# Software-pipelining the layer norm and transpose loop of a transformer layer on eight cores

## The chip, the cores and the metric

The kernel runs as one program on the 8 cores of a Trainium2 chip, without communication between the cores. The metric is the device time in microseconds of the slowest core. Each core has its own engines: TensorE (PE, with weight loads shown as PEld), VectorE (DVE), ScalarE (ACT), GpSimd (POOL, which here only issues the weight DMAs) and SyncE (SP, which issues the loads of activations and constants).

## What is computed

One transformer layer: attention on a layer norm of x, then a gated feed-forward network on a layer norm of the result, each with a residual. The reference, cut to what matters here:

```python
def _layernorm(x, axis=-1, eps=1e-5):
    m = jnp.mean(x, axis=axis, keepdims=True)
    v = jnp.var(x, axis=axis, keepdims=True)
    return (x - m) / jnp.sqrt(v + eps)

    x = L0_attn_x                       # (4, 2048, 2048) f32
    x = x + _L0_attn_ref(_layernorm(x, axis=-1), Wq, Wk, Wv, Wo)   # 16 heads, 4 KV heads, rope, alibi, causal
    x = x + _L0_ffn_ref(_layernorm(x, axis=-1), ...)               # router over 64, 8 groups, silu(g) * u, down
    return x
```

Each core takes one batch element and half of its 128-row query blocks. It normalises all 2048 tokens of its batch element, since it needs K and V of all of them.

## The kernel before

The program is written as lists of instructions per engine, which a small class collects: `p.emit` and `p.inc` append an instruction to an engine's list ("te", "ve", "se", "gp", "sy"), `p.inc` also increments that engine's semaphore and returns the count reached, `p.wait` makes an engine wait for such a count, and `p.dma` issues a load (its line in the profile is always L182). Each engine works its list strictly in the order of the calls, so the order in which `build` is written is the order of every queue.

The stages are: layer norm and transposition of x into XLN (bf16, features on the partitions); the K projection with rope (L436), the V projection (L491), the Q projection (L542); attention (`build_p2`); the output projection and the second layer norm (`build_p3`, which loads half of x_perm once more and transposes it); the feed-forward network over 8 groups (`build_p4`), which ends with transposes and stores (L1299).

The change touches the first stage alone. It runs over 16 tiles `tt` of 128 tokens, each in two halves `hc` of 1024 features. There are four load buffers XL of 128 x 1024 f32, so two tiles; half hc of tile tt uses XL[(2*tt + hc) % 4]. The columns of the small statistics are kept four-fold (`par = tt % 4`). For each tile, in the order of the queues:

- SP loads both halves, once VectorE has normalised out of that buffer and ScalarE's Exp of that tile is done (`ve_xl_free`, `se_xl_free`).
- ScalarE sums each half (L338, Copy with accumulate); VectorE squares and accumulates each half (L344).
- VectorE makes mean and variance in five instructions on one column (L349, L352, L355, L358, L361).
- ScalarE makes 1/sqrt(var + eps) as Ln (L366) and Exp (L369); VectorE makes -mean times that (L372).
- For each half: VectorE normalises it into XLNORMP[par % 2] (L382), TensorE transposes it in eight blocks of 128 x 128 f32 into PS[2 + hc] (L392), and ScalarE casts the result into XLN (L401, a CAST row). XLNORMP has two buffers, but a tile uses the one picked by its parity for both of its halves, so the second half is normalised after the first half's transposes. VectorE also waits for the transposes behind each half.

The K projection needs the casts of four tiles for each of its four column blocks (`evac_done`), and its weights in WKV, which POOL loads (two of four before the first stage ends).

Of the kernel before, what the change touches and what calls it, by code (L numbers as in the profile page):

```python
# [189 lines left out]
def build(taps=(), upto=4, sub=99):  # L190
    nc = bass.Bass("TRN2", target_bir_lowering=False)
# [21 lines left out]
    out = nc.dram_tensor("out", [TOWN, D], F32, kind="ExternalOutput").ap()  # L213
# [7 lines left out]
    def f32v(off_b, n):  # L221
# [19 lines left out]
    XL   = [f32v(163840, 1024), f32v(167936, 1024),  # L241
            f32v(65536, 1024), f32v(69632, 1024)]
# [12 lines left out]
    XLNORMP = [f32v(192512, 1024), f32v(196608, 1024)]  # L255
# [9 lines left out]
    IDNF  = f32v(cst(512), 128)  # L265
# [13 lines left out]
    SCR  = f32v(cst(256), 64)  # L279
# [4 lines left out]
    p = Prog(nc)  # L284
# [17 lines left out]
    se_xl_free = [0, 0, 0, 0]  # L302
    te_norm_free = [0, 0]
    cS0, cS1, cQ0, cQ1, cSUM, cSQ, cM, cMSQ, cVAR, cR, cNMR, cTMP = range(12)
    cEPS = 62

    def scr(col):
        return SCR[:, col:col + 1]
# [9 lines left out]
    prev_nv_tok = [0, 0]  # L318
    tpose_done = []
    evac_done = []  # L320
    last_norm_te = 0
    for tt in range(16):
        par = tt % 4
        def scr(col, par=None, _S=SCR):
            return _S[:, col:col + 1]
        def scrp(col, par):
            return SCR[:, 12 * par + col:12 * par + col + 1]
        for hc in (0, 1):
            slot = (tt * 2 + hc) % 4
            p.wait("sy", "VE", ve_xl_free[slot])  # L330
            p.wait("sy", "SE", se_xl_free[slot])
            xld.append((f"LX{slot}", p.dma("sy", XL[slot], x_r[tt, hc], sem=f"LX{slot}")))
        for hc in (0, 1):
            slot = (tt * 2 + hc) % 4
            p.wait("se", *xld[tt * 2 + hc])
            p.wait("se", "VE", prev_ve_tok[par])
            p.wait("se", "SE", prev_sq_tok[par])
            rtok = p.inc("se", lambda s_, sl=slot, par=par, c=(cS0, cS1)[hc]: s_.activation(  # L338
                HJUNK, XL[sl], AF.Copy, accum_out=scrp(c, par)), "SE")
            prev_sq_tok[par] = rtok  # L340
            p.wait("ve", *xld[tt * 2 + hc])
            p.wait("ve", "VE", prev_rtok[par])
            sq_tok = p.inc("ve", lambda v, sl=slot, par=par, c=(cQ0, cQ1)[hc]:
                v.scalar_tensor_tensor(  # L344
                    out=VJUNK, in0=XL[sl], scalar=1.0, in1=XL[sl],
                    op0=ALU.mult, op1=ALU.mult, accum_out=scrp(c, par)), "VE")
            prev_rtok[par] = sq_tok
        p.wait("ve", "SE", rtok)
        t1 = p.inc("ve", lambda v, par=par: v.tensor_tensor(  # L349
            out=scrp(cSUM, par), in0=scrp(cS0, par), in1=scrp(cS1, par), op=ALU.add), "VE")  # L350
        p.wait("ve", "VE", sq_tok)
        t2 = p.inc("ve", lambda v, par=par: v.tensor_tensor(  # L352
            out=scrp(cSQ, par), in0=scrp(cQ0, par), in1=scrp(cQ1, par), op=ALU.add), "VE")
        p.wait("ve", "VE", t1)
        t3 = p.inc("ve", lambda v, par=par: v.tensor_scalar(out=scrp(cM, par), in0=scrp(cSUM, par),  # L355
                   scalar1=1.0 / D, scalar2=None, op0=ALU.mult), "VE")
        p.wait("ve", "VE", t3)
        t4 = p.inc("ve", lambda v, par=par: v.tensor_scalar(out=scrp(cMSQ, par), in0=scrp(cM, par),  # L358
                   scalar1=scrp(cM, par), scalar2=None, op0=ALU.mult), "VE")
        p.wait("ve", "VE", t4)  # L360
        ve_tok = p.inc("ve", lambda v, par=par: v.scalar_tensor_tensor(  # L361
            out=scrp(cVAR, par), in0=scrp(cSQ, par), scalar=1.0 / D, in1=scrp(cMSQ, par),
            op0=ALU.mult, op1=ALU.subtract), "VE")
        prev_ve_tok[par] = ve_tok
        p.wait("se", "VE", ve_tok)
        s1 = p.inc("se", lambda s_, par=par: s_.activation(scrp(cTMP, par), scrp(cVAR, par), AF.Ln,  # L366
                   bias=scr(cEPS)), "SE")
        p.wait("se", "SE", s1)
        se_tok = p.inc("se", lambda s_, par=par: s_.activation(scrp(cR, par), scrp(cTMP, par), AF.Exp,  # L369
                       scale=-0.5), "SE")  # L370
        p.wait("ve", "SE", se_tok)
        ve_tok = p.inc("ve", lambda v, par=par: v.tensor_scalar(  # L372
            out=scrp(cNMR, par), in0=scrp(cM, par), scalar1=scrp(cR, par), scalar2=-1.0,
            op0=ALU.mult, op1=ALU.mult), "VE")
        p.wait("ve", "VE", ve_tok)
        p.wait("se", "VE", ve_tok)
        for hc in (0, 1):
            slot = (tt * 2 + hc) % 4
            se_xl_free[slot] = se_tok
            p.wait("ve", "TE", te_norm_free[par % 2])  # L380
            p.wait("ve", "VE", prev_nv_tok[par % 2])
            nv_tok = p.inc("ve", lambda v, sl=slot, par=par: v.tensor_scalar(  # L382
                out=XLNORMP[par % 2], in0=XL[sl], scalar1=scrp(cR, par), scalar2=scrp(cNMR, par),
                op0=ALU.mult, op1=ALU.add), "VE")
            prev_nv_tok[par % 2] = nv_tok
            ve_xl_free[slot] = nv_tok
            p.wait("te", "VE", nv_tok)
            ps = PS[2 + hc]
            if len(evac_done) >= 2:
                p.wait("te", "SE", evac_done[-2])  # L390
            for j in range(8):
                fn = (lambda t_, j=j, ps=ps, par=par: nc.tensor.transpose(  # L392
                    ps[:, j * 128:(j + 1) * 128],
                    XLNORMP[par % 2][:, j * 128:(j + 1) * 128], IDNF))
                if j == 7:
                    te_norm_free[par % 2] = p.inc("te", fn, "TE")
                else:
                    p.emit("te", fn)
            p.wait("ve", "TE", te_norm_free[par % 2])
            p.wait("se", "TE", te_norm_free[par % 2])  # L400
            ev = p.inc("se", lambda s_, ps=ps, hc=hc, tt=tt: s_.copy(  # L401
                out=XLN.rearrange("p (hh q) -> p hh q", q=2048)[:, hc * 8:hc * 8 + 8,
                    tt * 128:(tt + 1) * 128],
                in_=ps.rearrange("p (a b) -> p a b", b=128)), "SE")
            evac_done.append(ev)
    p1a_te = p.cnt["TE"]; p1a_ve = p.cnt["VE"]
    taps_avail["XLN"] = (XLN, BF16, "SE", p.cnt["SE"])
    q_rope_done = kv_rope_done = 0
# [2 lines left out]
    if sub >= 1:  # L411
# [11 lines left out]
        for c in range(4):  # L423
            slot = c % 2
# [6 lines left out]
            for tc in range(4):  # L431
                if c == 0:
                    p.wait("te", "SE", evac_done[(tc * 4 + 3) * 2 + 1])
                ps = PS[tc // 2]
                for hh in range(16):
                    fn = (lambda t_, hh=hh, tc=tc, ps=ps, sl=slot: nc.tensor.matmul(  # L436
                        ps[:, (tc % 2) * 512:(tc % 2) * 512 + 512],
                        WKV[sl][:, hh * 128:(hh + 1) * 128],
                        XLN[:, hh * 2048 + tc * 512: hh * 2048 + tc * 512 + 512],
                        start=(hh == 0), stop=(hh == 15)))  # L440
# [5 lines left out]
            for ch in range(2):  # L446
                psK = PS[ch]
                psW = PS[2 + ch]
                sl = slice(ch * 1024, ch * 1024 + 1024)
# [4 lines left out]
                se_tok = p.inc("se", lambda s_, psK=psK: s_.copy(out=RAW, in_=psK[:]), "SE")  # L454
# [3 lines left out]
                for half_ in range(2):  # L458
                    fn = (lambda t_, psW=psW, half_=half_: nc.tensor.matmul(
                        psW[:, half_ * 512:half_ * 512 + 512], JROT,  # L460
                        RAW[:, half_ * 512:half_ * 512 + 512], start=True, stop=True))
# [5 lines left out]
                    out=VTTF[:, 0:1024], in0=RAW, in1=COS2K[:, sl], op=ALU.mult), "VE")  # L467
                p.wait("ve", "TE", jtok)
                sm_tok = p.inc("ve", lambda v, psW=psW, sl=sl: v.tensor_tensor(
                    out=VTTF[:, 1024:2048], in0=psW[:], in1=SIN2K[:, sl], op=ALU.mult), "VE")  # L470
                p.wait("ve", "VE", sm_tok)
                ev = p.inc("ve", lambda v, c=c, sl=sl: v.tensor_tensor(
                    out=KT[:, c * 2048 + sl.start: c * 2048 + sl.stop],
                    in0=VTTF[:, 0:1024], in1=VTTF[:, 1024:2048], op=ALU.add), "VE")
# [5 lines left out]
        for c in range(4 if sub >= 2 else 0):  # L480
            slot = c % 2
# [6 lines left out]
            for tc in range(4):  # L488
                ps = PS[tc // 2]
                for hh in range(16):  # L490
                    fn = (lambda t_, hh=hh, tc=tc, ps=ps, sl=slot: nc.tensor.matmul(  # L491
                        ps[:, (tc % 2) * 512:(tc % 2) * 512 + 512],
                        WKV[sl][:, hh * 128:(hh + 1) * 128],
                        XLN[:, hh * 2048 + tc * 512: hh * 2048 + tc * 512 + 512],
                        start=(hh == 0), stop=(hh == 15)))
# [11 lines left out]
            for grp in (0, 1):  # L507
                ps = PS[2 + grp]
                for j in range(8):
# [6 lines left out]
                    else:  # L516
# [3 lines left out]
                    out=VTOK.rearrange("p (tt f) -> p tt f", f=512)[:, grp * 8:grp * 8 + 8,  # L520
                        c * 128:(c + 1) * 128],
# [9 lines left out]
        for h in range(NH if sub >= 3 else 0):  # L531
            slot = h % 2
# [805 lines left out]
```

How the kernel before makes its waits and increments, by code:

```python
    def inc(self, eng, fn, sem, n=1):  # L165
        self.cnt[sem] += n
        h = self.sem[sem]
        self.ops[eng].append(lambda e, fn=fn, h=h, n=n: fn(e).then_inc(h, n))
        return self.cnt[sem]
# [1 line left out]
    def wait(self, eng, sem, val):  # L171
        if val <= 0:
            return
        h = self.sem[sem]
        self.ops[eng].append(lambda e, h=h, v=val: e.wait_ge(h, v))
```

## Time and profile before

| | us |
|---|---|
| median of 2 runs | 3482.24 (3478.38 to 3486.09) |
| profiled execution | 3484.57 |
| its span on the slowest core (core 2) | 3483.0 |
| spans of the other cores | 3459.6 to 3471.1 |
| TensorE, busy in the span | 2939.4 (84%) |
| VectorE | 1045.2 (30%) |
| ScalarE | 432.8 (12%) |
| GpSimd | 385.3 (11%) |

The page divides the span into 40 slices of 87 us. TensorE is busy 2, 3 and 5 tenths in the first three and mostly 7 to 9 tenths after that. In the rows, a time such as 203.37 is us from the start of the span, the number behind it is the duration, "xN" the number of instructions merged into a row, and the bracket tells how long the engine stood idle before the row and what ended the wait. L numbers are lines of the kernel before. AR is the one large SBUF tensor that all buffers are cut from, PS is PSUM. Rows are of core 2, the slowest, unless a group names another. Of the matmul records a few per cent can be missing, so a merged matmul row can have a count that is short by one or two.

### The profile page before, as it was taken

How to read it: one execution, taken by the hardware profiler on the slowest of the kernel's cores; microseconds unless marked ns; L12 is line 12 of the kernel's file. 1: busy time of each engine (PE TensorE's matmuls, PEld its weight loads, DVE VectorE, ACT ScalarE, POOL GpSimd, SP SyncE). 2: the span in 40 equal slices, each digit the busy share in tenths (PEclk: the TensorE clock that was granted, in tenths of full speed). 3: DMA queues.
4: the chain of work that ended last, by engine and by line, in shares of the span. 5: the costliest groups of instructions: out<-in, count | busy, mean ns of one | idle time of the engine just before them, and what ended most of it. 6: DMA issues, size and time to landing. Idle time of an engine off the chain costs nothing.

```text
span 3483.0 us, 33988 instructions; the slowest of 8 cores (3459.6 to 3483.0 us)
## 1 busy us (share of the span) xinstructions
PE 2939.4 (84%) x12367; PEld 1317.6 (38%) x12602; DVE 1045.2 (30%) x1358; ACT 432.8 (12%) x663; POOL 385.3 (11%) x350
## 2 busy tenths in 40 slices
PE   2356787788765997899999999999999999999986
PEld 1222332122233456343443443443443433434434
DVE  2433134433452125313214114123123123133123
ACT  2320011233453110000000000000000000000000
POOL 0000010000000100111111111111111111111110
PEclk9998897555786995899999999999999999999997
DMA  5312264000002620787676676776775876776744
GB/s 130 88 36 25 19 60 46 1 1 13 1 1 85 67 24 5 69 80 68 65 73 67 67 78 59 69 77 63 73 73 55 81 71 60 73 74 63 76 46 122
DMA packets 640647, 200.52 MB, mean 58 GB/s; under 512 B 632027, under 2 KB 632540, under 8 KB 639206
## 3 DMA queue, kind: packets, MB, share of 16 engines
q0 software_dynamic: 628208, 159.67, 47.6%
q1 hardware_dynamic: 12278, 38.67, 3.8%
q8 instruction: 105, 1.72, 0.2%
q14 instruction: 56, 0.46, 0.1%
HBM read 349.57 MB, written 8.39 MB: 103 GB/s over the span
## 4 chain that ended last, share of the span: by engine, by line
PE 73%; DMA 9%; DVE 8%; issue 5%; ACT 4%; DVEq 0%; SPq 0%; ACTq 0%; POOLq 0%
PE PS L1215 17%; PE PS L1209 17%; PE PS L1260 13%; DMA AR<-downT 6%; PE PS L542 3%; DVE AR L779 3%; PE PS L768 3%; PE PS L773 2%; PE PS L869 2%; PE PS L436 2%; PE PS L392 2%; PE PS L491 2%; PE PS L960 2%; PE PS L1169 1%; DMA AR<-x_perm 1%
## 5 line engine op out<-in xcount | busy, mean ns | idle before, releaser
L1209 PE MATMUL PS<-AR 128*128 128x512 bf16 x2759 | 826.2, 379 | 4.9 <-DVE AR L1176 1.9
L1215 PE MATMUL PS<-AR 128*128 128x512 bf16 x2760 | 826.4, 379 | 3.0
L1260 PE MATMUL PS<-AR 128*128 128x512 bf16 x2755 | 649.0, 390 | 39.6 <-DMA AR<-downT 25.5
L1260 PEld LDWEIGHTS PS<-AR 128*128 128x128 bf16 x2816 | 273.3, 100 | 416.2 <-issue 127.2
L1234 DVE TENSOR_TENSOR AR<-PS,AR 128x1024 bf16<-128x1024 f32 x88 | 107.7, 1224 | 1009.1 <-ACT AR L1229 1009.1
L1209 PEld LDWEIGHTS PS<-AR 128*128 128x128 bf16 x2816 | 275.7, 98 | 335.1 <-issue 3.5
L1215 PEld LDWEIGHTS PS<-AR 128*128 128x128 bf16 x2816 | 275.7, 98 | 333.1 <-issue 1.4
L1229 ACT ACTIVATE AR<-PS 128x1024 bf16<-128x1024 f32 x88 | 90.1, 1024 | 1811.7 <-PE PS L1215 1811.7
L1272 DVE TENSOR_TENSOR AR<-AR,PS 128x1024 f32<-128x1024 f32 x128 | 156.3, 1221 | 468.7 <-PE PS L1260 468.7
L768 PE MATMUL PS<-AR 128*128 128x512 bf16 (+3 forms) x355 | 153.2, 433 | 101.7 <-DVE AR L756 99.8
L747 ACT ACTIVATE AR<-PS,AR 128x384 bf16<-128x384 f32 (+3 forms) x365 | 198.5, 577 | 306.3 <-PE PS L717 127.5
L182 POOL DMA_DIRECT2D AR<-gateT x88 | 100.8, 1145 | 1032.9 <-PE PS L1215 1022.8
L182 POOL DMA_DIRECT2D AR<-downT x128 | 137.1, 1071 | 666.4 <-PE PS L1169 484.9
L392 PE MATMUL PS<-AR 128*128 128x128 f32 x256 | 62.1, 424 | 160.4 <-DVE AR L382 141.9
L773 PE MATMUL PS<-AR 128*128 128x512 bf16 (+3 forms) x363 | 162.1, 451 | 5.6 <-DVE PS L731 3.3
L1176 DVE TENSOR_TENSOR AR<-PS,AR 128x1024 bf16<-128x1024 f32 x128 | 154.3, 1217 | 3.5 <-PE PS L1169 3.3
L756 DVE TENSOR_TENSOR AR<-AR 128x128 bf16<-128x128 bf16 x365 | 75.7, 223 | 248.3 <-ACT AR L747 246.4
L869 PE MATMUL PS<-AR 128*128 128x512 bf16 x501 | 113.3, 383 | 5.2 <-DMA AR<-Wo 4.4
L542 PE MATMUL PS<-AR 128*128 128x512 bf16 x502 | 115.3, 386 | 2.2 <-DVE AR L519 1.7
L768 PEld LDWEIGHTS PS<-AR 128*128 128x128 bf16 x365 | 39.9, 109 | 201.9 <-issue 194.6
L779 DVE RECIPROCAL AR<-PS 128x512 f32<-128x512 f32 x32 | 107.4, 3357 | 26.8 <-PE PS L773 26.8
L392 PEld LDWEIGHTS PS<-AR 128*128 128x128 f32 x256 | 50.2, 223 | 171.9 <-issue 171.9
(124 smaller groups left out, 1848.2 us busy)
## 6 DMA issues: line engine op xcount, KB each, us to landing
AR<-gateT POOLq DMA_DIRECT2D x88, 512.0 KB, 6.3
AR<-upT POOLq DMA_DIRECT2D x88, 512.0 KB, 8.2
AR<-downT POOLq DMA_DIRECT2D x128, 352.0 KB, 5.3
AR<-x_perm SPq DMA_DIRECT2D x48, 512.0 KB, 4.5
AR<-Wq POOLq DMA_DIRECT2D x16, 512.0 KB, 8.5
AR<-Wo POOLq DMA_DIRECT2D x16, 512.0 KB, 6.5
out<-AR SPq DMA_DIRECT2D x8, 1024.0 KB, 3.9
AR<-Wk POOLq DMA_DIRECT2D x4, 512.0 KB, 9.0
```

The source lines that it names most:

```text
L182: return self.inc(q, lambda e, o=out, i=in_: e.dma_start(out=o, in_=i), sem, 16)
L392: fn = (lambda t_, j=j, ps=ps, par=par: nc.tensor.transpose(ps[:, j * 128:(j + 1) * 128], XLNORMP[par % 2][:, j * 128:(j + 1) * 128], IDNF))
L542: fn = (lambda t_, hh=hh, tc=tc, ps=ps, sl=slot: nc.tensor.matmul(ps[:, tc * 512: tc * 512 + 512], WSL[sl][:, hh * 128:(hh + 1) * 128], XL ...
L747: ncols=ncols, sl6=sl6: s_.activation(PSB[sl6][:, 0:ncols], scs[:, 0:ncols], AF.Exp, bias=ALIBIK[:, h * 16 + kp: h * 16 + kp + 1], scale=C ...
L768: ncolsj=ncolsj, first=first, last=last: nc.tensor.matmul(OS[:, 128 * sj:512], VTOK[:, (kpj * 4 + kv) * 128:(kpj * 4 + kv + 1) * 128], PSB ...
L773: ncolsj=ncolsj, first=first, last=last: nc.tensor.matmul(OS[:, 512 + 128 * sj:1024], ONESBF, PSB[sl4j][:, 0:ncolsj], start=first, stop=la ...
L779: r1 = p.inc("ve", lambda v, OS=OS: v.reciprocal(out=RECIPB, in_=OS[:, 512:1024]), "VE")
L869: fn = (lambda t_, dh=dh, tc=tc, ps=ps, sl=slot: nc.tensor.matmul(ps[:, tc * 512:tc * 512 + 512], WSL[sl][:, dh * 128:(dh + 1) * 128], OT[ ...
L1209: fn = (lambda t_, hh=hh, tc=tc, psG=psG, sl=sg: nc.tensor.matmul(psG[:, tc * 512:(tc + 1) * 512], GSL[sl][:, hh * 128:(hh + 1) * 128], XG ...
L1215: fn = (lambda t_, hh=hh, tc=tc, psU=psU, sl=su: nc.tensor.matmul(psU[:, tc * 512:(tc + 1) * 512], USL[sl][:, hh * 128:(hh + 1) * 128], XG ...
L1260: fn = (lambda t_, it=it, tc=tc, psD=psD, sl=sd: nc.tensor.matmul(psD[:, tc * 512:(tc + 1) * 512], DSL[sl][:, it * 128:(it + 1) * 128], AP ...
L1272: x2_add[hh] = p.inc("ve", lambda v, hh=hh, psD=psD: v.tensor_tensor(out=X1T[:, hh * 1024:(hh + 1) * 1024], in0=X1T[:, hh * 1024:(hh + 1) ...
```

## The change

The loop over tiles is split into four functions, and these are called in a skewed order. `emit_load` issues the loads of a tile, `emit_stats_sums` ScalarE's two sums, `emit_stats` VectorE's squares, the small statistics, Ln and Exp, and `emit_finish` the rest: -mean times rstd, the normalisation, the transposes and the casts. Step s of the new loop issues the sums of tile s, the finish of tile s-1, the loads of tile s+1, and then the statistics of tile s.

In `emit_finish` half hc is normalised into XLNORMP[hc], and both normalisations are issued before the transposes. VectorE's waits for the transposes behind each half are gone; it waits for the transposes of the tile before when it overwrites XLNORMP[hc]. TensorE waits for the cast of the tile before in the same PSUM tile (`evac_prev[hc]`), as it did. SP's wait for ScalarE before a buffer is loaded anew is now for the sum of that half and no longer for the tile's Exp; ScalarE's wait for -mean times rstd ahead of the casts is dropped.

The diff, cut to its core (the statements inside the functions that are not shown are the same):

```diff
-    for tt in range(16):
-        par = tt % 4
...
+    def emit_load(tt):
         for hc in (0, 1):
             slot = (tt * 2 + hc) % 4
             p.wait("sy", "VE", ve_xl_free[slot])
             p.wait("sy", "SE", se_xl_free[slot])
             xld.append((f"LX{slot}", p.dma("sy", XL[slot], x_r[tt, hc], sem=f"LX{slot}")))
+
+    def emit_stats_sums(tt):
+        par = tt % 4
...
+            rtok_t[tt][hc] = rtok
+            se_xl_free[slot] = rtok
+
+    def emit_stats(tt):
...
+        exp_tok[tt] = se_tok
+
+    def emit_finish(tt):
+        par = tt % 4
+        p.wait("ve", "SE", exp_tok[tt])
...
-        p.wait("ve", "VE", ve_tok)
-        p.wait("se", "VE", ve_tok)
+        p.wait("ve", "VE", nmr_tok)
         for hc in (0, 1):
             slot = (tt * 2 + hc) % 4
-            se_xl_free[slot] = se_tok
-            p.wait("ve", "TE", te_norm_free[par % 2])
-            p.wait("ve", "VE", prev_nv_tok[par % 2])
-            nv_tok = p.inc("ve", lambda v, sl=slot, par=par: v.tensor_scalar(
-                out=XLNORMP[par % 2], in0=XL[sl], scalar1=scrp(cR, par), scalar2=scrp(cNMR, par),
+            p.wait("ve", "TE", te_norm_free[hc])
+            nv_tok = p.inc("ve", lambda v, sl=slot, par=par, hc=hc: v.tensor_scalar(
+                out=XLNORMP[hc], in0=XL[sl], scalar1=scrp(cR, par), scalar2=scrp(cNMR, par),
                 op0=ALU.mult, op1=ALU.add), "VE")
-            prev_nv_tok[par % 2] = nv_tok
+            prev_nv_tok[hc] = nv_tok
             ve_xl_free[slot] = nv_tok
+        for hc in (0, 1):
+            nv_tok = prev_nv_tok[hc]
             p.wait("te", "VE", nv_tok)
             ps = PS[2 + hc]
-            if len(evac_done) >= 2:
-                p.wait("te", "SE", evac_done[-2])
+            p.wait("te", "SE", evac_prev[hc])
...
-            p.wait("ve", "TE", te_norm_free[par % 2])
-            p.wait("se", "TE", te_norm_free[par % 2])
+            p.wait("se", "TE", te_norm_free[hc])
...
+            evac_prev[hc] = ev
             evac_done.append(ev)
+
+    emit_load(0)
+    emit_load(1)
+    for step in range(17):
+        if step < 16:
+            emit_stats_sums(step)
+        if step >= 1:
+            emit_finish(step - 1)
+        if step >= 1 and step + 1 < 16:
+            emit_load(step + 1)
+        if step < 16:
+            emit_stats(step)
```

## Rows read from the trace of the kernel before

**Rows 1.** Windows view: us, busy time (instructions) of PE, PEld, DVE, ACT, POOL; clock, DMA share, GB/s.
```profile
27.67:222.70 195.03, 62.10 (x256) 50.49 (x258) 81.59 (x193) 75.99 (x129) 0.00 (x0) 1.00 0.33 84
```

**Rows 2.** Waits, 27 to 235 us: who waited for whom, us in total, times, longest.
```profile
PE PS L392 <- DVE AR L382: 141.9, 18, 36.5
ACT AR L401 <- PE PS L392: 94.6, 32, 3.8
DVE AR L382 <- PE PS L392: 39.5, 16, 2.9
DVE AR L344 <- PE PS L392: 36.3, 15, 2.5
```

**Rows 3.** Timeline, 150 to 330 us: one tile's round on core 2.
```profile
198.48 1.01 ACT L401 CAST AR<-PS 128x1024 bf16<-128x1024 f32 x1 [2.24 <-PE PS L392]
198.63 1.22 DVE L344 SCALAR_TENSOR_TENSOR AR<-AR 128x1024 f32<-128x1024 f32 x1 [2.44 <-PE PS L392]
199.39 1.06 ACT L338 ACTIVATE AR<-AR 128x1024 f32<-128x1024 f32 x1
...
199.97 1.22 DVE L344 SCALAR_TENSOR_TENSOR AR<-AR 128x1024 f32<-128x1024 f32 x1
...
200.63 1.06 ACT L338 ACTIVATE AR<-AR 128x1024 f32<-128x1024 f32 x1
201.12 0.08 DVE L344 DVE_READ_ACCUMULATOR AR<-AR 128x1 f32 x1
...
201.88 0.16 DVE L349 TENSOR_TENSOR AR<-AR 128x1 f32<-128x1 f32 x1 [0.68 <-ACT AR L338]
...
202.98 0.29 ACT L366 ACTIVATE AR<-AR 128x1 f32<-128x1 f32 x1 [1.20 <-DVE AR L361]
203.37 0.20 ACT L369 ACTIVATE AR<-AR 128x1 f32<-128x1 f32 x1
203.68 0.21 DVE L372 TENSOR_SCALAR AR<-AR 128x1 f32<-128x1 f32 x1 [0.79 <-ACT AR L369]
204.14 0.81 DVE L382 TENSOR_SCALAR AR<-AR 128x1024 f32<-128x1024 f32 x1 [0.24 <-DVE AR L372]
...
205.20 1.94 PE L392 MATMUL PS<-AR 128*128 128x128 f32 x8 [6.81 <-DVE AR L382]
207.23 1.01 ACT L401 CAST AR<-PS 128x1024 bf16<-128x1024 f32 x1 [3.66 <-PE PS L392]
...
208.45 1.94 PE L392 MATMUL PS<-AR 128*128 128x128 f32 x8 [1.31 <-ACT AR L401]
210.49 1.01 ACT L401 CAST AR<-PS 128x1024 bf16<-128x1024 f32 x1 [2.24 <-PE PS L392]
```

**Rows 4.** Timeline, core 2: the first tile's Exp and the last group of transposes.
```profile
34.95 0.20 ACT L369 ACTIVATE AR<-AR 128x1 f32<-128x1 f32 x1
...
220.54 1.94 PE L392 MATMUL PS<-AR 128*128 128x128 f32 x8 [1.39 <-ACT AR L401]
```

**Rows 5.** Timeline, core 0, 205 to 224 us: last transposes, then the K projection.
```profile
219.60 1.94 PE L392 MATMUL PS<-AR 128*128 128x128 f32 x8 [1.39 <-ACT AR L401]
...
221.34 2.84 PE L436 MATMUL PS<-AR 128*128 128x512 bf16 x7
```

**Rows 6.** Tile view of x_perm, 0 to 235 us: its 32 loads of this stage.
```profile
DMA to landing us min/median/max: 3.9/4.7/20.9
```

**Rows 7.** DMA view, 1075 to 1135 us: issues, KB each, median us to landing.
```profile
AR<-x_perm SPq DMA_DIRECT2D x14, 512.0 KB, 3.9
```

**Rows 8.** DMA view, 0 to 235 us: the K weights.
```profile
AR<-Wk POOLq DMA_DIRECT2D x2, 512.0 KB, 19.8
```

**Rows 9.** Timeline of PE: transposes in the V stage and in the output stage.
```profile
415.63 1.07 PE L511 MATMUL PS<-AR 128*128 128x128 f32 x8 [2.67 <-DVE AR L504]
...
3466.78 3.65 PE L1299 MATMUL PS<-AR 128*128 128x128 f32 x16 [2.61 <-DVE AR L1306]
```

**Rows 10.** Windows view of a part of the output stage.
```profile
3440.00:3470.00 30.00, 17.19 (x79) 15.86 (x80) 11.66 (x10) 0.00 (x0) 0.00 (x0) 0.56 0.43 179
```

More of the change, by code:

```diff
@@ L321, in build, with scr, scrp @@
     last_norm_te = 0
-    for tt in range(16):
-        par = tt % 4
[L324 to L327, printed above, removed]
+    evac_prev = [0, 0]
+    exp_tok = [0] * 16
+    rtok_t = [[0, 0] for _ in range(16)]
+    def scr(col, par=None, _S=SCR):
+        return _S[:, col:col + 1]
+    def scrp(col, par):
+        return SCR[:, 12 * par + col:12 * par + col + 1]
+    def emit_load(tt):
         for hc in (0, 1):
@@ L340, in build @@
             prev_sq_tok[par] = rtok
+            rtok_t[tt][hc] = rtok
[3 more added lines that the diff above has]
+        for hc in (0, 1):
+            slot = (tt * 2 + hc) % 4
             p.wait("ve", *xld[tt * 2 + hc])
@@ L347, in build @@
             prev_rtok[par] = sq_tok
+        rtok = rtok_t[tt][1]
         p.wait("ve", "SE", rtok)
@@ L370, in build @@
                        scale=-0.5), "SE")
-        p.wait("ve", "SE", se_tok)
-        ve_tok = p.inc("ve", lambda v, par=par: v.tensor_scalar(
+        exp_tok[tt] = se_tok
+    def emit_finish(tt):
+        par = tt % 4
+        p.wait("ve", "SE", exp_tok[tt])
+        nmr_tok = p.inc("ve", lambda v, par=par: v.tensor_scalar(
             out=scrp(cNMR, par), in0=scrp(cM, par), scalar1=scrp(cR, par), scalar2=-1.0,
             op0=ALU.mult, op1=ALU.mult), "VE")
-        p.wait("ve", "VE", ve_tok)
@@ L384, in build @@
                 op0=ALU.mult, op1=ALU.add), "VE")
-            prev_nv_tok[par % 2] = nv_tok
+            prev_nv_tok[hc] = nv_tok
             ve_xl_free[slot] = nv_tok
+        for hc in (0, 1):
+            nv_tok = prev_nv_tok[hc]
             p.wait("te", "VE", nv_tok)
             ps = PS[2 + hc]
-            if len(evac_done) >= 2:
-                p.wait("te", "SE", evac_done[-2])
+            p.wait("te", "SE", evac_prev[hc])
             for j in range(8):
-                fn = (lambda t_, j=j, ps=ps, par=par: nc.tensor.transpose(
+                fn = (lambda t_, j=j, ps=ps, hc=hc: nc.tensor.transpose(
@@ L393, in build @@
                     ps[:, j * 128:(j + 1) * 128],
-                    XLNORMP[par % 2][:, j * 128:(j + 1) * 128], IDNF))
+                    XLNORMP[hc][:, j * 128:(j + 1) * 128], IDNF))
                 if j == 7:
-                    te_norm_free[par % 2] = p.inc("te", fn, "TE")
+                    te_norm_free[hc] = p.inc("te", fn, "TE")
                 else:
                     p.emit("te", fn)
-            p.wait("ve", "TE", te_norm_free[par % 2])
-            p.wait("se", "TE", te_norm_free[par % 2])
+            p.wait("se", "TE", te_norm_free[hc])
```

## The prediction

> **What bounds the kernel now.** I read the page first: the span of 3483.0 us (3484.57 us with what lies around it) ends in matmul stages that the diff leaves alone. So I went to the stretch that the changed loop fills, from the first load's landing to the first matmul of the K projection. The row of that stretch [rows 1] is 195.03 us long, and in it TensorE is busy 62.10 us, VectorE 81.59 and ScalarE 75.99: no engine is busy for half of it, and the DMA share is 0.33. Nothing is at capacity here; the time is hand-overs. The waits of the same stretch [rows 2] say which: TensorE waits 141.9 us for the normalised halves (L382), ScalarE 94.6 us for transposes, VectorE 39.5 us for transposes before the second normalisation and 36.3 us before the next tile's squares. That is one tile at a time, going round all engines.
>
> The timeline of one tile [rows 3] shows the round. From one tile's second cast (198.48) to the next one's (210.49) is 12.01 us. In order: the sums and squares of both halves, the small statistics, Ln, Exp, -mean*rstd, normalise half 0 (204.14), transpose it (205.20), cast it (207.23), and only then the second half's transposes (208.45) and cast (210.49), because both halves share one XLNORMP buffer. The first Exp of the stage starts at 34.95 and the last group of transposes at 220.54 [rows 4]; behind that group the K projection starts without a gap, since on core 0 the next matmul starts 221.34 - 219.60 = 1.74 us after the last group did [rows 5]. So this stage's length enters the end one for one.
>
> **The change, step by step.** No arithmetic is added or dropped: the instructions are the same ones with the same shapes. What moves is (a) each half gets its own XLNORMP buffer, so both normalisations and both transpose groups follow one another; (b) ScalarE sums the next tile ahead of this tile's casts; (c) VectorE squares the next tile behind this tile's normalisations, while TensorE transposes. I place a tile's instructions from the start of the Exp of the tile before, called t = 0; every term is a start-to-start difference in [rows 3] unless another group is named.
>
> - Path through TensorE. Exp to -mean*rstd 0.31 (203.37 to 203.68); to normalise half 0: 0.46; to its transposes 1.06. So transposes of half 0 start at 1.83. The second group stands right behind it on TensorE, its input being ready: half 1 is normalised by about 0.77 + 2 x 0.81 = 2.39. A group followed by more work takes 1.74 us on core 0 [rows 5], so it starts at 3.57. Transposes to cast 2.03 (205.20 to 207.23): the second cast starts at 5.60. Cast to the next ScalarE instruction 0.91 (198.48 to 199.39): Ln at 6.51. Ln to Exp 0.39: the next Exp at 6.90.
> - Path through VectorE. The squares of the next tile start at about 2.39, the second square 1.34 later at 3.73 (198.63 to 199.97). The first of the small instructions follows the second square by 1.91 now (199.97 to 201.88), but it waits there for ScalarE's sums; the accumulator read starts 1.15 after the square (201.12) and I put the small chain at 1.25 behind the square, 4.98. Small chain to Ln 1.10 (201.88 to 202.98): 6.08. That is 0.43 before ScalarE is free, so VectorE doesn't set the period. With the whole 1.91 it would be 6.74, a period of 7.13; this is my upper bound for that step.
> - ScalarE. The two sums start at about 0.2 and 1.44 (199.39 to 200.63 is 1.24) and are read out by 2.6, before the first cast can start at 1.83 + 2.03 = 3.86. Standing ahead of the casts they cost nothing, as long as their data is there. If this cover went, each microsecond over 1.26 would hold the first cast, and over about 2 the second.
> - Loads. On SP's queue the loads of tile s+1 wait for the normalisations of tile s-1 and for its sums, as before. The first is free at about t = 1.6 and has its data after the median of 4.7 us at 6.3; it is wanted by the sum at 6.90 + 0.2 = 7.1. The second is free at 2.4, lands at 7.1 and is wanted at 8.3. The worst landing, 20.9 us, belongs to the first loads, which queue behind the constants [rows 6]. The rate asked for is 1.05 MB per 6.90 us, 152 GB/s; a later stage loads the same x_perm blocks two at a time and its 14 loads landed in 3.9 us at the median [rows 7], so I take 4.7 and not more. SP has nothing else queued in this stage.
> - POOL. It issues nothing in the stage. The K weights are now wanted some 79 us earlier, at about 144 us; their first two loads are issued ahead of the stage and took 19.8 us [rows 8]. Cost nothing.
>
> So the period falls from 12.01 to 6.90 us. Fifteen periods after 34.95 the last Exp starts at 138.45; the last group of transposes starts 3.57 later at 142.02, where it started at 220.54. The saving is 78.5 us, and since the K projection follows directly and the rest is unchanged, the profiled execution would be 3484.57 - 78.5 = 3406.1 us. The median of the runs is 2.3 us under the profiled execution, so the forecast is **3404 us**, 2.3% less.
>
> One thing could move this path: TensorE's clock. A group of eight takes 1.94 us here, 1.07 us in the V stage at 415.63 [rows 9], and the K projection's first matmuls on core 0 come about 0.43 us apart, seven in 2.84 us [rows 5], so this stage works at the lower of the two levels (1.2 GHz), though the granted clock of its stretch prints 1.00 [rows 1]. The new loop has TensorE in work some 3.66 of 6.90 us, 53%. The nearest row is the output stage: sixteen transposes in 3.65 us, 2.61 us idle, thus 58% in work, and a granted clock of 0.56, mostly the lower level [rows 9, 10]. I therefore keep the lower level. The Trainium skill ("TensorE: Matmul & The Clock Gate", Part 4: PE-mode transpose) says that transposes do not count towards the full clock as matmuls do; by that rule the sum above stands. The same page's Part 1 says that the low clock is the default and activity releases it; by that one the first rival below would hold. The output stage's row agrees more with the former.
>
> **Rivals.**
> - *The clock rises.* Both groups then take about 1.07 us, the casts are done by about 5, and VectorE's 6.08 + 0.39 = 6.47 us becomes the period. The last transposes would end near 34.95 + 15 x 6.47 + 1.83 + 2.0 = 135.8 instead of 222.5, and ten first matmuls of the K projection gain about 0.2 each: 89 us saved, 3393 us against the median. For it: the density of TensorE's work rises from a third to a half. Against it: the 0.56 at 58%.
> - *Loads become the bound.* A buffer goes free, is loaded for L, is summed (0.2 + 2.5), cast behind it (1.9), Ln and Exp (0.4 and handover), then normalised (1.6): two periods = L + 6.6. At L = 4.7 that asks only 5.7 us, and from L = 7.2 it decides. If eight cores loading at twice the density double the landing to 9.4, the period is 8.0 us, the saving 78.5 - 15 x 1.1 = 62 us, and the time 3420 us, within 2%. For it: two loads are now in flight within 0.8 us of each other. Against it: the 3.9 us in the stage with the same rate.
> - *The overlap is worth less than the starts say*, because waits on semaphores that are now spread over a shorter period take time that today hides behind others. The VectorE bound of 7.13 costs 3.5 us; a period of 7.5 costs 9 us and gives 3413 us, the border of 2%.
> - *Slower than before.* ScalarE's queue is in order, and the next tile's sums now stand ahead of this tile's casts. A late load so holds the casts, these hold PSUM and Ln, and the stage could pass 12.01 us per tile; by the same formula this needs L above 24.0 - 6.6 = 17.4 us, with 18 us it would be 12.3 us per tile and 3487 us. Only loads behind the constants took so long (20.9).
> - *The order doesn't overlap at all* would need the buffers to be shared still; the two XLNORMP halves exclude that.
>
> **How the numbers follow.** Forecast 0.72, with its own range of 3399 to 3411 (period 6.6 to 7.4). Clock rises 0.09. Loads bound or overlap worth less, past 7.4 us per tile: 0.16, most of it between 3412 and 3422. Slower 0.02, and 0.01 for anything I don't see, counted as slower. The range takes the clock's 3393 and ends at 3416. A measurement of this kernel can tell about 2% from no change, that is below 3412.6 us: faster 0.80, same 0.17, slower 0.03.
>
> **What would show it.** In the changed kernel's timeline the second casts should be 6.9 us apart; the two transpose groups of a tile touch, and the first matmul of the K projection starts near 143.8 us instead of 222. TensorE's waits for L382 should shrink from 141.9 us to about 50 and ScalarE's idle time should lie before the casts. VectorE should wait for Exp before -mean*rstd, not for TensorE. Wrong would be: ScalarE or VectorE waiting for x_perm beyond the first tile (loads), groups of eight taking 1.07 us (clock), Ln waiting for the small chain (VectorE as the bound), or later stages that differ in length.

## The result

| | before | changed |
|---|---|---|
| profiled execution | 3484.57 us | 3403.09 us |
| its span, slowest core | 3483.0 us | 3401.5 us |
| ratio of the times | | 0.9749, 95% interval 0.9727 to 0.9771 |
| the same, measured again later (e7) | | 0.9767, 0.9725 to 0.9809 |
| median of all executions | 3505.05 us (10) | 3480.25 us (11) |

The change makes the kernel 2.5% faster (2.3% in the second measurement, whose interval goes from 1.9 to 2.8%). The last row can only be read with this: about half of the executions of either kernel were disturbed, with the cores of one die at a lower clock and up to 400 us longer, so the medians say little and the ratio compares the undisturbed ones. Applied to the 3482.24 us of the prediction, the ratio gives 3394.8 us.

The changed kernel's page. Its first lines, and the group of the transposes (line, engine, operation, count; busy us, mean ns; idle before and its releaser):

```profile
span 3401.5 us, 34145 instructions; the slowest of 8 cores (3385.5 to 3401.5 us)
PE 2943.2 (87%) x12602; PEld 1319.3 (39%) x12602; DVE 1041.0 (31%) x1358; ACT 432.3 (13%) x663; POOL 385.0 (11%) x350
...
L410 PE MATMUL PS<-AR 128*128 128x128 f32 x256 | 58.3, 423 | 84.2 <-DVE AR L399 74.8
```

Windows view of its first stage, the stretch that answers to [rows 1] (us, busy time of PE, PEld, DVE, ACT, POOL, granted clock, DMA share, GB/s):

```profile
27.65:142.36 114.71, 58.12 (x256) 52.52 (x257) 77.58 (x193) 75.70 (x128) 0.00 (x0) 1.00 0.48 141
```

The stretch is 80.3 us shorter, 114.71 us for 195.03, with the same instructions and nearly the same busy times: VectorE 77.58 us for 81.59, ScalarE 75.70 for 75.99. Nearly all that went is idle time. The waits of the changed kernel, 27 to 150 us, answer to [rows 2]:

```profile
PE PS L410 <- DVE AR L399: 74.8, 13, 36.8
ACT AR L418 <- PE PS L410: 30.0, 32, 3.6
...
DVE AR L392 <- ACT AR L385: 22.1, 16, 1.5
PE PS L410 <- ACT AR L346: 9.5, 3, 3.2
DVE AR L359 <- DMA AR<-x_perm: 3.2, 2, 2.3
DVE AR L399 <- DVE AR L392: 2.7, 15, 0.2
ACT AR L346 <- DMA AR<-x_perm: 2.0, 6, 0.5
```

VectorE no longer waits for transposes at all (39.5 and 36.3 us before); ScalarE waits 30.0 us for them instead of 94.6. VectorE's wait for Exp ahead of -mean*rstd was there before and has grown, to 22.1 us and at most 1.5 us a tile. In the waits of the kernel before, 27 to 235 us, it was

```profile
DVE AR L372 <- ACT AR L369: 12.6, 16, 0.8
```

New are the 2.0 us in which ScalarE waits for x_perm. The round of one tile, from the timeline of core 7 (start, duration), answers to [rows 3]:

```profile
62.27 0.20 ACT L385 ACTIVATE AR<-AR 128x1 f32<-128x1 f32 x1
62.46 1.06 ACT L346 ACTIVATE AR<-AR 128x1024 f32<-128x1024 f32 x1
62.58 0.21 DVE L392 TENSOR_SCALAR AR<-AR 128x1 f32<-128x1 f32 x1 [1.45 <-ACT AR L385]
62.97 1.53 DVE L399 TENSOR_SCALAR AR<-AR 128x1024 f32<-128x1024 f32 x2 [0.18 <-DVE AR L392]
...
64.03 3.65 PE L410 MATMUL PS<-AR 128*128 128x128 f32 x16 [3.15 <-DVE AR L399]
...
64.42 1.22 DVE L359 SCALAR_TENSOR_TENSOR AR<-AR 128x1024 f32<-128x1024 f32 x1
...
65.75 1.23 DVE L359 SCALAR_TENSOR_TENSOR AR<-AR 128x1024 f32<-128x1024 f32 x1
66.06 1.01 ACT L418 CAST AR<-PS 128x1024 bf16<-128x1024 f32 x1 [0.78 <-PE PS L410]
66.90 0.08 DVE L359 DVE_READ_ACCUMULATOR AR<-AR 128x1 f32 x1
66.90 0.15 DVE L365 TENSOR_TENSOR AR<-AR 128x1 f32<-128x1 f32 x1
...
67.77 1.01 ACT L418 CAST AR<-PS 128x1024 bf16<-128x1024 f32 x1 [0.69 <-PE PS L410]
67.77 0.16 DVE L377 SCALAR_TENSOR_TENSOR AR<-AR 128x1 f32<-128x1 f32 x1
68.67 0.30 ACT L382 ACTIVATE AR<-AR 128x1 f32<-128x1 f32 x1
69.06 0.20 ACT L385 ACTIVATE AR<-AR 128x1 f32<-128x1 f32 x1
```

From Exp to Exp it is 6.79 us. Both transpose groups are one run of sixteen in 3.65 us, and VectorE squares the next tile (64.42) while they run. The variance (67.77) is done while the second cast is at work, so Ln (68.67) waits for ScalarE and not for VectorE.

The table below splits all traces at the first matmul of each stage, mean over the eight cores, in us. "First stage" is from the first transpose to the first matmul of the K projection; "behind it" is from there to the core's end, with its range over the cores.

| trace | first stage | behind it | mean span |
|---|---|---|---|
| before, shown | 185.8 | 3247 (3236 to 3260) | 3469.5 |
| before, e8 | 185.9 | 3254 (3240 to 3270) | 3475.6 |
| before, e9 | 185.9 | 3250 (3234 to 3269) | 3471.2 |
| changed, shown | 105.5 | 3252 (3244 to 3259) | 3393.8 |
| changed, e7 | 105.0 | 3247 (3227 to 3263) | 3388.4 |
| changed, e10 | 104.8 | 3254 (3238 to 3271) | 3394.3 |
| e1, two buffers, no skew | 157.7 | 3236 (3229 to 3246) | 3428.9 |
| e2, skew, one buffer | 133.5 | 3244 (3233 to 3261) | 3413.6 |
| e3, late loads | 121.1 | 3237 (3229 to 3243) | 3394.5 |
| e4, two tiles loaded | 105.0 | 3247 (3233 to 3270) | 3387.9 |
| e5, Ln and Exp first | 96.0 | 3245 (3236 to 3265) | 3377.3 |
| e6, lag of two | 80.1 | 3251 (3234 to 3277) | 3370.4 |
| e11, the same again | 80.2 | 3246 (3237 to 3267) | 3364.8 |

The mean of the first stage repeats within 1 us between traces of the same kernel (its cores differ by 0.5 us before and by about 2 us in the changed kernel's later traces); what stands behind it scatters by some 40 us between cores. All effects below are therefore read from the first stage, and the totals are given beside it. In the lag-of-two kernels the first transpose starts 2.8 us later than in the changed kernel, and they are compared by the start of the K projection.

### The profile page after: what moved, and what is told of

It reads as the page before. It is cut to its first block, busy times and chain, and to the rows that moved or that the text cites. A ratio compares the mean times of both kernels' runs of the same rounds, so it can differ in the third digit from the quotient of the medians.

```text
span 3401.5 us, 34145 instructions; the slowest of 8 cores (3385.5 to 3401.5 us)
## 1 busy us (share of the span) xinstructions
PE 2943.2 (87%) x12602; PEld 1319.3 (39%) x12602; DVE 1041.0 (31%) x1358; ACT 432.3 (13%) x663; POOL 385.0 (11%) x350
## 4 chain that ended last, share of the span: by engine, by line
PE 76%; DMA 9%; DVE 8%; issue 4%; ACT 3%; SPq 0%; DVEq 0%; ACTq 0%; POOLq 0%
PE PS L1239 18%; PE PS L1245 18%; PE PS L1290 14%; DMA AR<-downT 6%; PE PS L572 3%; PE PS L798 3%; DVE AR L809 3%; PE PS L803 2%; PE PS L899 2%; PE PS L521 2%; PE PS L466 2%; PE PS L990 2%; PE PS L410 2%; PE PS L1199 2%; DMA AR<-x_perm 2%
## 5 line engine op out<-in xcount | busy, mean ns | idle before, releaser
L798 PE MATMUL PS<-AR 128*128 128x384 bf16 (+3 forms) x365 | 159.6, 438 | 103.8 <-DVE AR L786 102.7
L803 PE MATMUL PS<-AR 128*128 128x384 bf16 (+3 forms) x365 | 162.2, 450 | 0.0
L410 PE MATMUL PS<-AR 128*128 128x128 f32 x256 | 58.3, 423 | 84.2 <-DVE AR L399 74.8
L1269 DVE TENSOR_TENSOR AR<-AR 128x1024 bf16<-128x1024 bf16 x88 | 107.8, 1225 | 16.6 <-DVE AR L1264 16.6
```

The lines of the kernel that those rows point to most:

```text
L798: ncolsj=ncolsj, first=first, last=last: nc.tensor.matmul(OS[:, 128 * sj:512], VTOK[:, (kpj * 4 + kv) * 128:(kpj * 4 + kv + 1) * 128], PSB ...
L803: ncolsj=ncolsj, first=first, last=last: nc.tensor.matmul(OS[:, 512 + 128 * sj:1024], ONESBF, PSB[sl4j][:, 0:ncolsj], start=first, stop=la ...
```

## The experiments

**e1: two buffers, no skew.** The two ways in which the change acts are taken apart. Theory: the period is the longest chain of hand-overs, and the skew brings most of the gain.

```diff
-    for step in range(17):
...
+    for tt in range(16):
+        emit_stats_sums(tt)
+        emit_stats(tt)
+        emit_finish(tt)
+        if tt + 2 < 16:
+            emit_load(tt + 2)
```

> Part (a) of the change alone: each half has its own XLNORMP buffer and both halves are normalised before the transposes, but the tiles are not skewed, so the next tile's sums stand behind this tile's casts on ScalarE (the order of steps is sums, statistics, finish of the same tile). Theory (the period is the longest chain of hand-overs, and the skew carries most of the gain): second cast to the small chain 3.40 us, to Ln 1.10, to Exp 0.39, to -mean*rstd 0.31, to normalise 0.42, to transposes 1.04, two groups 1.71, to the cast 2.03: period 10.40 us, last transposes about 24 us earlier than before and about 53 us later than in the changed kernel; total about 3459 us (0.993 of before). Rival (the two buffers carry the gain, the order of the sums is incidental): period near 6.8 to 7.5 us and a total near 3400 us.

Ratio 0.9918 (0.9867 to 0.9968), where 0.993 was expected. ScalarE in the timeline of core 5, one round:

```profile
90.69 1.01 ACT L418 CAST AR<-PS 128x1024 bf16<-128x1024 f32 x1 [0.50 <-PE PS L410]
91.60 1.06 ACT L346 ACTIVATE AR<-AR 128x1024 f32<-128x1024 f32 x1
92.84 1.06 ACT L346 ACTIVATE AR<-AR 128x1024 f32<-128x1024 f32 x1
95.19 0.29 ACT L382 ACTIVATE AR<-AR 128x1 f32<-128x1 f32 x1 [1.20 <-DVE AR L377]
95.58 0.20 ACT L385 ACTIVATE AR<-AR 128x1 f32<-128x1 f32 x1
99.37 1.01 ACT L418 CAST AR<-PS 128x1024 bf16<-128x1024 f32 x1 [3.59 <-PE PS L410]
100.91 1.01 ACT L418 CAST AR<-PS 128x1024 bf16<-128x1024 f32 x1 [0.52 <-PE PS L410]
```

The second casts are 10.22 us apart (10.40 expected), and the sums stand behind them. The two casts are 1.54 us apart here and not 1.71: the granted clock of the stage is 0.68 in this trace, which shortens some transposes. The stage is 28 us shorter than before and 53 us longer than changed: without the skew a third of the gain is left. The rival, that they carry it, is out.

What e1 takes away is less than its expectation says. Its order of calls gives VectorE, TensorE and SP the same queues as the changed kernel; only ScalarE's sums of the next tile move, behind this tile's casts. VectorE's waits for transposes are gone here too, and it squares the next tile while TensorE transposes (97.73 us, with the transposes at 97.34). So e1 has the prediction's points (a) and (c), and against the changed kernel it prices (b) alone, at 53 us. Waits of core 5, 27 to 200 us: VectorE's small chain stands and waits for the sums.

```profile
DVE AR L365 <- ACT AR L346: 61.1, 16, 4.4
```

**e2: skew, one buffer.** The changed kernel without point (a).

```diff
-            p.wait("ve", "TE", te_norm_free[hc])
+            p.wait("ve", "TE", te_norm_free[par % 2])
...
-                out=XLNORMP[hc], in0=XL[sl], ...
+                out=XLNORMP[par % 2], in0=XL[sl], ...
...
             ve_xl_free[slot] = nv_tok
-        for hc in (0, 1):
-            nv_tok = prev_nv_tok[hc]
             p.wait("te", "VE", nv_tok)
```

(The transposes read XLNORMP[par % 2] too, and each half's transposes stand right behind its normalisation.)

> Parts (b) and (c) alone: the skewed order of the changed kernel, but both halves of a tile share one XLNORMP buffer by parity as before, so half 1 is normalised only after the transposes of half 0. Theory: Exp, -mean*rstd 0.31, normalise half 0 0.39, transposes 1.04, normalise half 1 2.19 later, squares 0.72, second square 1.33, small chain 1.15, Ln 1.13, Exp 0.39: the chain through VectorE becomes the longest, period 8.65 us; the one through TensorE would give 8.3. Saving over before about 3.36 x 15 = 50 us, total about 3431 us (0.986). VectorE should be seen waiting for transposes (L of the normalisation) in every tile. Rival (the buffers don't matter once the order is skewed): 6.8 us and about 3400 us.

Ratio 0.9841 (0.9786 to 0.9896), where 0.986 was expected. The timeline's second casts, and VectorE's wait from the waits of the stage:

```profile
92.51 1.01 ACT L416 CAST AR<-PS 128x1024 bf16<-128x1024 f32 x1 [2.11 <-PE PS L408]
93.75 0.29 ACT L382 ACTIVATE AR<-AR 128x1 f32<-128x1 f32 x1 [0.23 <-DVE AR L377]
...
101.05 1.01 ACT L416 CAST AR<-PS 128x1024 bf16<-128x1024 f32 x1 [2.11 <-PE PS L408]
```

```profile
DVE AR L399 <- PE PS L408: 36.8, 16, 2.4
```

The period is 8.54 us (8.65 expected), and Ln now waits for VectorE's variance, as the sum had it: the chain through VectorE is the longest one here. Half 1 waits for the transposes of half 0 in all 16 tiles. Points (b) and (c) give 52 us of the 81, and the second buffer the other 28, as much as (a) and (c) give in e1. So the buffer is worth 28 us and the order of the sums 53, each on top of the rest. Point (c) is in both e1 and e2, and no run has it alone; that the two prices fill the 81 us suggests that it is worth nothing by itself. The rows of before fit that, though they don't show it: the first small instruction waits 0.68 us for ScalarE's sums there and not for the squares [rows 3].

**e3: loads issued late.** Is the cover of the loads real, and what is it worth?

```diff
         if step >= 1 and step + 1 < 16:
+            p.wait("sy", "VE", prev_ve_tok[step % 4])
             emit_load(step + 1)
```

(The loads are also emitted behind the statistics, so that this token is the one of tile s.)

> The changed kernel with one wait more on SP: the loads of tile s+1 are issued only when the variance of tile s is done, some 3.5 to 4 us later than the buffers are free. Theory (loads are hidden in the changed kernel, and with the cover gone they set the period): variance, load 4.5 to 4.7, first square 1.33, second 1.15, small chain 1.0: 8.0 to 8.3 us per tile, ScalarE and VectorE waiting for x_perm in every tile; total about 20 us over the changed kernel, 3420 to 3428 us. Rival (loads have slack of more than 4 us): 6.8 us per tile, no change.

Timeline of core 3, where both engines wait for the load:

```profile
83.31 1.22 DVE L359 SCALAR_TENSOR_TENSOR AR<-AR 128x1024 f32<-128x1024 f32 x1 [1.83 <-DMA AR<-x_perm]
83.34 1.06 ACT L346 ACTIVATE AR<-AR 128x1024 f32<-128x1024 f32 x1 [3.89 <-DMA AR<-x_perm]
...
91.10 1.06 ACT L346 ACTIVATE AR<-AR 128x1024 f32<-128x1024 f32 x1 [3.06 <-DMA AR<-x_perm]
```

The period is 7.76 us in this round and 7.9 us at the mean of this core's rounds (8.0 to 8.3 expected), and the stage is 16 us longer than changed (20 expected): with the cover gone the loads set the period. The median from issue to landing was 4.3 us in this trace, shorter than the 4.5 to 4.7 I had put in. The time of this one execution, 3400.5 us, lies under the expected 3420 to 3428: the stages behind took 3237 us at the mean, 10 to 17 us less than in the changed kernel's traces, which hides it.

**e4: no loads behind the second tile.** The other end of the same question. `emit_load` returns the tokens of the first two tiles for all later ones; tiles 2 to 15 are computed from stale data.

> The changed kernel without the 28 loads of tiles 2 to 15: the buffers keep the first two tiles, so the work of the engines is the same and the values are not (this part of the computation is left out). Theory (loads cost the changed kernel nothing): period 6.80 us as with the loads, last transposes at the same time within 1 us; ScalarE's waits of 0.15 to 0.5 us for x_perm vanish without shortening anything. Rival (the loads set the period in part): a period under 6.7 us and the stage more than 2 us shorter.

The first stage is 105.0 us, as with the loads, and sixteen transposes start every 6.80 us:

```profile
117.49 3.65 PE L414 MATMUL PS<-AR 128*128 128x128 f32 x16 [3.15 <-DVE AR L403]
124.29 3.65 PE L414 MATMUL PS<-AR 128*128 128x128 f32 x16 [3.15 <-DVE AR L403]
```

So the 2.0 us that ScalarE waits for x_perm in the changed kernel cost nothing. Its loads landed in 5.5 us at the median, against 4.7 before [rows 6]; the cover held that.

**e5: Ln and Exp ahead of the second cast.** If the second cast before Ln is what sets 6.80 us, moving Ln ahead must shorten it down to VectorE's chain.

```diff
+            if hc == 1 and defer_cast:
+                held.append((tt, te_norm_free[1]))
+                continue
             p.wait("se", "TE", te_norm_free[hc])
...
         if step < 16:
             emit_stats(step)
+        if step >= 1:
+            emit_cast1()
```

(`emit_cast1` issues the held cast of tile s-1.)

> The changed kernel with one move in ScalarE's queue: Ln and Exp of tile s stand ahead of the second cast of tile s-1. Theory (in the changed kernel the bound is the chain transposes, second cast, Ln; VectorE's chain is 0.6 us shorter): Exp, 0.31, 0.39, both normalisations 1.45, squares 1.33 + 1.15, small chain to Ln 1.13, Exp 0.39: 6.15 us per tile; 15 x 0.65 = 10 us less than the changed kernel, about 3385 to 3393 us. Ln then waits for the variance and not for the cast. Rival (the bound is VectorE or the loads already): 6.8 us, no change; or slower, if the held second cast delays the next transposes.

ScalarE, timeline of core 2:

```profile
83.16 0.29 ACT L382 ACTIVATE AR<-AR 128x1 f32<-128x1 f32 x1 [0.96 <-DVE AR L377]
83.55 0.20 ACT L385 ACTIVATE AR<-AR 128x1 f32<-128x1 f32 x1
83.66 0.99 ACT L434 CAST AR<-PS 128x1024 bf16<-128x1024 f32 x1
...
89.31 0.29 ACT L382 ACTIVATE AR<-AR 128x1 f32<-128x1 f32 x1 [0.96 <-DVE AR L377]
```

6.15 us, as expected to the hundredth; Ln waits for the variance. The stage is 9 us shorter than changed (10 expected). The time was missed: the four executions took 3394.9 to 3401.8 us, where 3385 to 3393 was expected. Their ratio, 0.9745 (0.9716 to 0.9774), could by itself not tell this kernel from the changed one; all cores average 3379.5 us against 3387.4 changed, 8 us less.

**e6 and e11: a lag of two tiles.** The same reasoning to its end: finish(s-2) between sums(s) and statistics(s), eight load buffers.

```diff
+            f32v(73728, 1024), f32v(77824, 1024),
+            f32v(81920, 1024), f32v(86016, 1024)]
...
-            slot = (tt * 2 + hc) % 4
+            slot = (tt * 2 + hc) % 8
...
+    for tt in range(4):
+        emit_load(tt)
+    for step in range(18):
+        if step < 16:
+            emit_stats_sums(step)
+        if step >= 2:
+            emit_finish(step - 2)
+            if step + 2 < 16:
+                emit_load(step + 2)
+        if step < 16:
+            emit_stats(step)
```

> The changed kernel with a lag of two tiles between statistics and finish instead of one, and eight load buffers instead of four (the added four lie where Q is written later). Theory (with no tile's Exp between the variance and its use, the period is VectorE's own work and issue): -mean*rstd 0.39, normalisations 1.45, squares 1.33 + 1.15, small chain 0.87 and 0.3 to the next: 5.4 to 5.5 us per tile; last transposes near 122 us of the span instead of 142, total 3375 to 3385 us, a ratio near 0.969. ScalarE is close behind with about 5.1 us of work per tile. Rival (loads at 1.05 MB per 5.4 us, 194 GB/s, become the bound): ScalarE and VectorE wait for x_perm, 6.5 us or more per tile and no gain over the changed kernel.

> The lag of two tiles with eight load buffers, timed once more. First stage 80 us (T to K) as in its first trace. Theory (its 25 us in the stage come through to the end, and only the scatter behind it hid them): ratio 0.969 to 0.971, clearly under the changed kernel's 0.975. Rival (the later stages give part of it back through a lower clock in the Q projection): 0.973 or more, again with a Q projection over 160 us on half of the cores.

Timeline of core 1:

```profile
75.65 1.53 DVE L401 TENSOR_SCALAR AR<-AR 128x1024 f32<-128x1024 f32 x2 [0.18 <-DVE AR L394]
...
76.72 1.94 PE L412 MATMUL PS<-AR 128*128 128x128 f32 x16 [1.66 <-ACT AR L387]
...
80.46 0.16 DVE L379 SCALAR_TENSOR_TENSOR AR<-AR 128x1 f32<-128x1 f32 x1
80.57 0.21 DVE L394 TENSOR_SCALAR AR<-AR 128x1 f32<-128x1 f32 x1
80.96 1.53 DVE L401 TENSOR_SCALAR AR<-AR 128x1024 f32<-128x1024 f32 x2 [0.18 <-DVE AR L394]
```

VectorE goes from the variance (80.46) to the next -mean*rstd (80.57) without a wait; the period is its own chain, 5.31 us (5.4 to 5.5 expected). The K projection starts at 119.0 us at the mean over the cores, where it was 141.1 in the changed traces: 22 us. No load is waited for behind the first tile, at 166 GB/s. The ratio is 0.972 both times (0.9685 to 0.9754; 0.9677 to 0.9763): ahead of the changed kernel's 0.9749 and 0.9767 by less than either interval. The comparable executions agree: their times average 3391.6 us (8 executions) against 3400.5 us (8), all cores 3369.2 against 3387.4, so 18 of the 22 us arrive on the average core. It is the fastest of these kernels, but my 0.969 to 0.971 was missed, and so was the time of 3375 to 3385 us: these executions took 3384.4 to 3402.2 us. The rival that the Q projection takes it back isn't borne out either: in e6 it took over 160 us on four cores, in e11 on two, at the same ratio.

**e7, e8, e9, e10: where the rest of the 87 us came from.** The ratio says 87 us, the trace of the stage 80 to 81. Is there a second gain, or, the other way round, does the long Q projection that some traces show give part of it back?

> The changed kernel itself once more beside the kernel before, on the chip and in the rounds of the others. The stage is shorter by 79 to 82 us in the traces, the ratio of the times says 87 us with an interval of 80 to 95. Theory (the whole gain is in the first stage, the rest is scatter of the stages behind it): ratio 0.977, within 0.9755 to 0.978. Rival (a second gain of 6 to 8 us in the later stages): 0.9749 again, with the stages behind the first one shorter on most cores.

> The kernel before itself, for a second trace. In four traces of changed kernels some cores take 174 us instead of 149 us for the Q projection, at a lower granted clock, which the first trace of the kernel before doesn't show. Theory (this is scatter of the clock that any kernel has): the stages behind the first one add up to 3230 to 3265 us on the cores here too, and some cores of this or the next trace show the long Q projection. Rival (the shorter, denser first stage brings it about and so gives back part of the gain): 149 to 151 us on all eight cores, and stages behind the first one of at most 3250 us.

> The kernel before, a third trace: as for the second one. With 24 cores seen, a share like that of the changed kernels (20 of 56 cores with a Q projection over 160 us) would show about 8; none would speak for the rival.

> The changed kernel, a third trace. First stage 105 us again on all cores (period 6.80 us). Theory (scatter of the clock): Q projection on 0 to 8 cores over 160 us, whole dies at a time. Rival (brought about by the change): over 160 us on at least four cores again.

e7 gave 0.9767, as its theory had it. Over the comparable executions whose core spans are on record, the mean span of the cores is 3468.3 us before (25 executions) and 3387.4 us changed (8), 80.9 us apart, and the first stage is 80.8 us shorter (185.9 against 105.1). There is no second gain: the time of the slowest core adds the scatter of what stands behind the first stage, and the clock in the Q projection, worth 22 us, is one part of it. That scatter can be seen in the kernel before as well, for instance in the Q projection of e9, core 6 and core 0:

```profile
486.69 8.58 PE L542 MATMUL PS<-AR 128*128 128x512 bf16 x32
```

```profile
485.50 7.07 PE L542 MATMUL PS<-AR 128*128 128x512 bf16 x32
```

Sixteen such heads take 171 us on cores 6 and 7 and 149 to 152 us on the other six. In e8 it is cores 4 and 5 (167 and 166 us), in the changed kernel's e7 four cores (173 to 174), in its first and third trace none over 155. So it is 4 of 24 cores over 160 us in either kernel, and the rival that the change brings it about is not supported; with three traces of each, a shift in how often it comes can't be excluded. The share of 20 in 56 cores in the expectation of e9 was a miscount: e1 to e7 have 14 such cores of 56, which would make 6 of 24. The theory of e10, whole dies at a time, doesn't hold: it is cores 0, 1, 4 and 5 in e7 and a single pair in e8 and e9.

## Why the prediction was right or wrong

The time recorded for the changed kernel, the median over all executions, is 3480.25 us and lies outside 3393 to 3416. The step that fails is the last one of the sum, from the profiled execution to the median of the runs. I put it at 2.3 us ("the median of the runs is 2.3 us under the profiled execution") because I took the two runs shown of before, 3478 and 3486 us, for the whole spread, and had no term for executions that are longer for other reasons than the code. Measured, the changed kernel's median lies 77.2 us above its profiled execution (3480.25 against 3403.09) and that of before 20.5 us above (3505.05 against 3484.57); ten runs of before reached 3884 us. So the medians are 24.8 us apart, where I had 78. The sum up to that step held: 3406.1 us forecast for the profiled execution, 3403.09 measured. By the ratio the time is 3394.8 us, inside the range, 9 us under the forecast of 3404, and the direction and the 2% were as forecast.

- **What bounds it.** Right. Hand-overs, not engines: with the same work, e1 gives 28 us and e2 52.
- **The path through TensorE, 6.90 us.** Measured 6.80. The one term off is -mean*rstd to normalise: 0.39 us and not 0.46, and 0.03 us at the transposes. The touching groups are as said: sixteen in 3.65 us, second cast 1.71 behind the first.
- **The path through VectorE.** Right that it doesn't set the period, with either of my values too long. The squares start 2.15 us behind Exp (62.27 to 64.42) and not 2.39, the small chain 1.15 us behind the second square (65.75 to 66.90) and not 1.25 or 1.91. e5 shows what the path is worth once it is alone: 6.15 us, where the rival of the rising clock had 6.47.
- **ScalarE's sums ahead of the casts.** Right: the first cast waits for TensorE and not for them (66.06, 0.78 us idle). e1, which differs from the changed kernel by having them behind the casts, loses 53 us.
- **Loads.** Right that they are hidden, and the slack was smaller than I wrote: landing took 5.5 us and not 4.7. I had kept 4.7 for the sake of the later stage with 3.9 us [rows 7] and called its rate the same; the windows view of the kernel before gives 123 GB/s for those 60 us, where I had worked out 152 for the changed stage. My sign of failure, any wait of ScalarE for x_perm, was too strict: it waits 2.0 us in all and e4 shows that they are free. What e3 adds is the price without cover, 16 us.
- **The stage.** 78.5 us forecast, 80.8 measured; 1.5 us of the difference come from the shorter period (15 x 0.10).
- **TensorE's waits.** I said about 50 us, the view has 74.8 + 9.5 us: I left out the 36.8 us before the first transpose, which the 141.9 us of before include too. Without it 47.5.
- **The clock.** In the changed kernel's trace it stayed at the lower level on core 7 (sixteen transposes in 3.65 us), so this rival did not set the time. The argument that took the output stage's clock over because of its share of work didn't hold in later traces, see below.

## What to carry to other kernels

Where no engine of a stage is busy for half of it, follow one item through the start times of all engines and add up start-to-start differences for the new order; here that gave the period of five out of six kernels within 3%, those of e1, e2, e5 and e6 with terms taken from the changed kernel's trace. In this case the order of one in-order queue was worth more than a buffer, 53 us against 28: put the next item's work ahead of the instruction that waits. And judge such a change by the stage in the traces of all cores, since 10 to 20 us of 3400 can't be seen in the slowest core's time.

## What was unexpected in the hardware

The clock rises for transposes too, and in these traces it doesn't follow TensorE's share of work. (The granted clock is the share of full speed that the profile gives for TensorE.) The windows of the first stage in four traces, of e10 (changed, core 0), e5 (core 2), e6 (core 1) and e1 (core 5):

```profile
36.00:141.00 105.00, 57.62 (x259) 51.54 (x260) 72.94 (x181) 70.89 (x120) 0.00 (x0) 0.61 0.49 141
```

```profile
36.00:132.00 96.00, 54.08 (x257) 48.86 (x259) 73.16 (x181) 68.86 (x120) 0.00 (x0) 0.72 0.48 154
```

```profile
36.00:119.00 83.00, 47.90 (x260) 43.06 (x261) 71.36 (x181) 69.31 (x120) 0.00 (x0) 0.77 0.55 166
```

```profile
36.00:190.00 154.00, 51.76 (x243) 48.57 (x244) 74.22 (x181) 70.75 (x120) 0.00 (x0) 0.68 0.33 96
```

TensorE is busy 55, 56, 58 and 34% of these, at a mean granted clock of 0.61, 0.72, 0.77 and 0.68. The clock switched between its two levels within the stage: in e6 the sixteen transposes at 76.72 take 1.94 us, those at 82.02 take 3.60 us. The Trainium skill ("TensorE: Matmul & The Clock Gate", Part 4) says the full clock doesn't engage for transposes; these traces show that it does at times. I had argued from the output stage's 0.56 at 58% that it would stay low at 53%; e1, at 34%, has 0.68. What starts a switch isn't shown. The stage hardly gains by it: in the changed kernel only a part of its groups is faster (103.9 to 106.0 us over the cores of its later traces), in e1 each group of sixteen still takes 3.30 to 3.50 us, so most of the time at the higher level lies between the groups, and in e6 VectorE is the bound. The granted clock also reads 1.00 in stretches where the same transposes take 3.65 us (the changed kernel's stage on core 7, and [rows 1] with 1.94 us for eight), so there it can't be taken at its word, and the durations decide.

The lower clock of the Q projection, 8.58 us for 32 matmuls where others take 7.07, comes in neighbouring pairs of cores (6 and 7 in e9, 4 and 5 in e8; two pairs at once in e6 and e7) and is neither of the two levels: the granted clock of such a stretch is 0.81.

```profile
400.00:450.00 50.00, 42.93 (x162) 17.01 (x161) 17.93 (x15) 5.06 (x5) 5.71 (x5) 0.81 0.55 53
```

(e7, core 0, windows view, in the Q projection; core 2 of the same execution has 1.00.)
